# Expert outputs written straight to token order by a slot table, plain loads at the end, expert pairs in the two row halves

## The reference

```python
# attention: 8 heads of 64 rows each here, 2048 x 2048 scores a head
q, k, v = x @ Wq + bq, x @ Wk + bk, x @ Wv + bv
weights = softmax(einsum('bdsh,bdth->bdst', q, k) / SCALE)
x = layernorm(x + einsum('bdst,bdth->bdsh', weights, v) @ Wo + bo)
# experts: 64 of them, each token goes to 6, an expert takes the first 256 rows
shared = silu(g_s) * y_s @ w_shared_down
pos = cumsum(one_hot(flat_e))[...] - 1;  valid = pos < CAP            # CAP = 256
x_disp = zeros((E, CAP, C)).at[flat_e, pos].set(x_flat[token_ids], mode='drop')
out_r = (silu(g_r) * v_r) @ w_down                                    # one expert: 256 x 64 @ 64 x 512
y_ts = where(valid, out_r[flat_e, pos], 0)
x = layernorm(x + shared + (y_ts.reshape(N, TOPK, C) * w).sum(axis=1))
```

## Time and profile before

| | us |
|---|---|
| median of 3 runs | 1485.49 |
| lowest, highest | 1482.91, 1488.73 |
| the profiled execution | 1479.0 |
| its span in the trace | 1477.3 |
| PE busy in the span | 1280.4 |
| DVE, ACT, POOL busy | 1059.5, 875.6, 598.6 |

### The profile page before, as it was taken

The page is one execution under the profiler, slowest core; times in us unless marked ns, Lnnn a source line. Parts: engine busy times, 40 slices in busy tenths (PEclk is TensorE's granted clock), DMA queues, the critical chain, the costliest instruction groups (busy, mean ns, idle before and its releaser), DMA issues. The chain is left out here.

```text
span 1477.3 us, 24021 instructions
## 1 busy us (share of the span) xinstructions
PE 1280.4 (87%) x8064; PEld 1068.7 (72%) x8064; DVE 1059.5 (72%) x1964; ACT 875.6 (59%) x1573; POOL 598.6 (41%) x588
## 2 busy tenths in 40 slices
PE   7999899999999999999999999869999999960000
PEld 6888799898898998998988989847666666630000
DVE  4523688799898897997988989746665656645665
ACT  4421589788787887886887868712555555530000
POOL 0002223245244344343443442523444444447785
PEclk9999999999999999999999999979999999985555
DMA  9998111122122122121221221246999999966665
GB/s 353 351 375 290 52 32 37 46 79 81 43 82 86 33 92 78 60 85 61 79 89 37 81 87 39 76 150 202 292 321 333 330 328 332 323 209 192 205 204 159
DMA packets 158374, 235.79 MB, mean 160 GB/s; under 512 B 14000, under 2 KB 102576, under 8 KB 158256
## 3 DMA queue, kind: packets, MB, share of 16 engines
q1 hardware_dynamic: 131920, 147.50, 31.9%
q0 software_dynamic: 24576, 83.88, 16.1%
q10 hardware_dynamic: 1760, 2.88, 0.6%
HBM read 118.89 MB, written 109.05 MB: 154 GB/s over the span
## 5 line engine op out<-in xcount | busy, mean ns | idle before, releaser
L674 ACT ACTIVATE p_hi<-slot 128x512 fp32r<-128x512 f32 x512 | 279.3, 596 | 108.3 <-PE slot L1146 98.8
L514 POOL TENSOR_TENSOR p_lo<-prob,p_hi 128x512 fp32r<-128x512 f32 x128 | 165.5, 1293 | 436.2 <-ACT prob L676 432.4
L1159 PE MATMUL slot<-k_stack,q_stack 128*128 128x512 f32 x1024 | 300.5, 416 | 4.5 <-POOL v_pair L455 4.5
L687 ACT ACTIVATE prob<-prob,row_min 128x1024 f32<-128x1024 f32 x256 | 296.3, 1158 | 8.6 <-DVE prob L940 8.6
L919 DVE TENSOR_TENSOR p_lo<-slot,p_hi 128x512 fp32r<-128x512 f32 x384 | 250.8, 681 | 44.0 <-ACT p_hi L674 42.6
L1178 PE MATMUL pv_acc<-p_hi,v_pair 128*128 128x256 f32 x1024 | 265.6, 292 | 3.8 <-POOL p_lo L514 3.2
L1146 PE MATMUL slot<-ident,prob 128*128 128x128 f32 x2048 | 265.2, 272 | 1.2 <-ACT prob L687 1.2
L1178 PE MATMUL pv_acc<-p_lo,v_pair 128*128 128x256 f32 x1024 | 255.2, 282 | 0.0
L1146 PEld LDWEIGHTS slot<-ident,prob 128*128 128x128 f32 x2048 | 230.9, 140 | 1.7 <-DVE prob L940 1.6
L1178 PEld LDWEIGHTS pv_acc<-p_hi,v_pair 128*128 128x128 f32 x1024 | 193.0, 189 | 17.9 <-issue 8.4
L1178 PEld LDWEIGHTS pv_acc<-p_lo,v_pair 128*128 128x128 f32 x1024 | 192.8, 188 | 11.7 <-issue 3.4
(11 more groups left out here) (133 smaller groups left out, 2041.7 us busy)
## 6 DMA issues: line engine op xcount, KB each, us to landing
disp_hbm<-zeros SPq DMA_DIRECT2D x64, 512.0 KB, 6.5
rows<-disp_hbm SPq DMA_DIRECT2D x64, 512.0 KB, 7.3
y_hbm<-y_out POOLq DMA_DIRECT2D x64, 512.0 KB, 7.1
q_stack<-q_hbm SPq DMA_DIRECT2D x128, 128.0 KB
up_w<-in_L_ffn_w_up SPq DMA_DIRECT2D x64, 256.0 KB, 4.4
down_w<-in_L_ffn_w_down SPq DMA_DIRECT2D x64, 128.0 KB, 5.2
stage<-in_L_attn_x SPq DMA_DIRECT2D x8, 512.0 KB, 9.4
q_hbm<-q_hi SPq DMA_DIRECT2D x8, 512.0 KB, 3.8
```

What stands on the lines that cost most here:

```text
L514: e.tensor_tensor(p_lo[1][:, 2:4, :], prob[:, m % 2, :, (4 * u + 2) * P:(4 * u + 4) * P], p_hi[1][:, 2:4, :].bitcast(F32), ALU.subtract).t ...
L674: e.activation(p_hi[b][:, two, :], view[:, two, :], ACT.Copy).then_inc(a_phi, 1)
L687: e.activation(keys, keys, ACT.Exp, bias=row_min[:, me % 2, j, 1:2], scale=-1.0, accum_out=row_sum[:, me % 2, j, half:half + 1]).then_inc( ...
L1159: made = e.matmul(slot[:, n * BANK:(n + 1) * BANK], qs[:, part, j * P:(j + 1) * P], k_stack[:, ms % H, keys], start=part == 0, stop=part == 1)
```

## The change

The names of lines below are those of the changed kernel.

- `y_hbm` becomes 12288 rows in token order (token x 6 + k). While POOL scatters a tile's rows to `disp_hbm`, it also writes with six more indirect DMAs (`note_rows`, L526), each of 128 values of 4 bytes, the number token x 6 + k into `table_hbm` at the same slot. In all 96 such DMAs are added. The table is first filled with an index out of bounds. At n = 6 SP waits for all of them and loads the table; at n = 7 PE turns it and DVE copies it to `row_at`.
- `place` waits for the `note_rows` of the last tile too (`d_tabw`). `keep_slots` is gone.
- `y_hbm` needs zeros, since an overflowed row is never written: 48 DMAs of 512 KB, one in every fourth step of the attention. The zeros of `disp_hbm` move: none ahead of the q stores, 32 behind them, and 32 in the first 32 steps of the attention. POOL waits for them ahead of its first scatter.
- Two experts make a pair. `hid` and `down_w` hold the first in partitions 0 to 63 and the second in 64 to 127. The down products of both are formed in the odd round, in four calls that alternate between the halves. The copies to `y_out` and the stores come then for both.
- The store of an expert is two indirect DMAs (L619), so a pair has four.
- Weights are loaded eight experts ahead (the first eight when the attention ends), rows seven items ahead.
- In the tail SP loads `got` with one plain DMA for each tile of tokens (L475: 6 rows a partition, 1.57 MB), four ahead. ACT scales two of the six rows, POOL adds these two (`part`), DVE does four products and one addition. DVE writes the norm in place, and SP stores from `base`.

The diff, cut to its core:

```diff
-        y_hbm = hbm("y_hbm", (E * CAP, C))
+        table_hbm = hbm("table_hbm", (E * CAP, 1))
+        y_hbm = hbm("y_hbm", (T * TOPK, C))
...
-        NB, NY = 5, 3
+        NB, NY = 8, 4
...
-            takes += [("down", n)] if n >= 0 else []
+            if 0 <= n < NS:
+                takes += [("down", n)] + ([("table", 0)] if n == NS - 1 else [])
+            elif n >= NS and n % 2:
+                takes += [("down", n - 1), ("down", n)]
...
-            for g in range(NS):
-                pieces = zero_some(2)
+            for g in range(E // 2):
+                e.dma_start(disp_pieces[g], zero_row).then_inc(d_zero, 16)
...
+                if s < E // 2:
+                    e.dma_start(disp_pieces[E // 2 + s], zero_row).then_inc(d_zero, 16)
+                elif s % 4 == 2 and E <= s < E + 4 * NZ:
+                    e.dma_start(y_pieces[(s - E) // 4], zero_row).then_inc(d_yzero, 16)
...
             attention_over(e)
+            for g in range(NB):
+                load_weights(e, g)
...
+            def note_rows(t, k):
+
+                e.indirect_dma_start(
+                    table_hbm, bass.IndirectOffsetOnAxis(scat[:, k:k + 1], 0), row_of[:, t, k:k + 1], None,
+                    bounds_check=E * CAP - 1, oob_is_err=False).then_inc(d_tabw, 16)
...
-                if n >= NS:
-                    g, y = n - NS, n % NY
-                    e.wait_ge(v_y, g + 1)
-                    e.wait_ge(a_y, g + 1)
-                    e.dma_start(y_rows[g], y_out[y][:, :, :]).then_inc(d_y[y], 16)
+                if n >= NS and n % 2:
...
+                    for i in (n - 1, n):
+                        g, y = i - NS, i % NY
+                        for t in range(2):
+                            e.wait_ge((v_y, a_y)[t], g + 1)
+                            e.indirect_dma_start(
+                                y_hbm, bass.IndirectOffsetOnAxis(row_at[:, 2 * g + t:2 * g + t + 1], 0),
+                                y_out[y][:, t, :], None, bounds_check=T * TOPK - 1,
+                                oob_is_err=False).then_inc(d_y[y], 16)
...
+                if u >= NG:
+                    e.wait_ge(v_acc, ACC * (u - NG + 1))
+                    e.wait_ge(g_part, u - NG + 1)
+                e.dma_start(got[u % NG][:, :, :], y_tiles[u]).then_inc(d_got[u % NG], 16)
+                if u >= NG:
+                    store_out(u - NG)
...
                 e.wait_ge(d_scat, 16 * TOPK * (2 * c + j))
+                e.wait_ge(d_tabw, 16 * TOPK * (2 * c + j))
...
+                elif n >= NS and n % 2:
...
+                    for t in range(2):
+                        for at, slot in two:
+                            made = e.matmul(slot[:, t * BANK:(t + 1) * BANK], hid[pair % 2][at, t * P:(t + 1) * P],
+                                            down_w[pair % (NB // 2)][at, :], start=True, stop=True)
+                            if t:
+                                made.then_inc(p_down, 1)
```

251 lines of the change are left out of this document (145 added, 106 removed).

## The result

The changed kernel takes 1626.64 us (median, 1625.70 to 1629.48) against 1486.14 us for the kernel before it (1482.91 to 1488.73). The ratio is 1.095, 95% interval 1.092 to 1.098: slower by 9.5%. The forecast was 1621 us. The medians differ by 140.5 us.

What follows compares the result with a forecast made beforehand. PE was taken to bound attention and experts, POOL's gathers the tail. Expert stage +140, tail -32, start +5.5, attention +11 and transition +11 gave +136 on 1485.5, so 1621 us, range 1545 to 1670.

Steps and rivals of the forecast that it cites:

- expert stage: A closed loop through POOL's four DMAs and `up_lo` makes a pair 13.5 us: 419 us against 278.5, +140.
- tail: After the experts: 14.2 us a pair of tiles, loads held behind stores on SP; 130 us against 161.8, -32.
- transition: Between attention and experts: notes delay tile 14's root, and `place` of tile 15 waits for notes; +11, between 3 and 16.
- start of the attention: 32 zeros on SP ahead of the first `q_stack` loads make these land later; +5.5, between 0 and 9.
- attention: Added indirect DMAs on POOL hold back `p_lo` by 1.9 us at the end of six chunks; +11, between 0 and 20.
- D: Expert stage: time of a pair's eight down matmuls on two row halves, taken as 2.4 us, bounds 1.98 and 3.70.
- The step on the clock: Expert stage: PE's clock falls after 4.3 us idle in each pair, costing 1.7 us, bounds 0 and 2.25.
- The high clock with full overlap: Rival in the expert stage: no clock loss, halves fully side by side, 11.4 us a pair; 1559 us, chance 0.19.
- No overlap: Rival in the expert stage: the row halves do not run side by side, 14.8 us a pair; 1660 us, chance 0.19.
- The short pitch: Rival in the expert stage: POOL issues the `y_out` DMAs in 0.25 us, PE binds; 1444 us, chance 0.05.
- The rival with the loads in time: Rival in the tail: loads arrive in time, 23 us less than the forecast; 1598 us, chance 0.05.
- The second wait: Transition: `place` of tile 15 waits until the notes of tile 14 land at 1020.6, 12.6 us later.

Runs made afterwards that it cites:

- e_same: Changed kernel with POOL's writes put behind `up_lo`, one expert a round, and both experts of a pair multiplied from the first row half: 1502.2 us.
- e_order_noalt: Changed kernel with POOL's writes put behind `up_lo`, one expert a round, and down calls ordered A, A, B, B instead of alternating: 1442.21 us.
- e_filler: Changed kernel plus 32 extra matmuls of PE ahead of its wait for the late `up_lo` of each pair: 1549.0 us.
- e_order: Changed kernel with POOL's indirect writes put behind the `up_lo` they held up, one expert a round: 1443.87 us, ratio 0.974 to the kernel before.
- e_tail: Changed kernel with SP issuing both loads of a pair of tail tiles before the stores of the pair two back: 1604.24 us.
- e_trans: Changed kernel with the last tile's input loaded ahead of SP's twelve weight loads, and POOL's last roots ahead of tile 13's notes: 1612.21 us.
- e_again: The changed kernel itself run again, nothing altered: 1615.94 us.
- e_best2: Changed kernel with new orders in experts, transition and tail, and the 32 zero writes ahead of `q_stack` moved into the attention's first 32 steps: 1415.61 us.
- e_half_inds: Changed kernel writing only the first 128 rows of each expert, one indirect write instead of two: 1510.79 us.

## Why the prediction was right, point by point

**The sum.** In us:

| term | forecast | measured | by |
|---|---|---|---|
| expert stage | +140 | +144.5 | stage windows |
| tail | -32 | -32.0 | stage windows |
| transition | +11 | +29.8 | stage windows; 9 to 11 of it are ScalarE's stalls |
| start of the attention | +5.5 | +3.9 | PE's start 157.55 to 161.45 |
| attention | +11 | +0.7 | stage windows |
| sum | +136 | +147.0 | spans |

The sum is closer than its terms, and that is luck in part: the transition was 19 us too low and the expert stage 4.5, the attention 10 too high and the start 1.6. Against the medians, which differ by 140.5 us, the forecast is 5 us off, and as far from the changed kernel run again (1615.9) on the other side.

**Expert stage: right, by the steps given.** The links came out as added up: the copy starts when the down pair ends, POOL's DMAs at a pitch of 1.28, `up_lo` 1.28. Two sizes inside were off and cancel: D is 1.99 us at full clock where I took 2.4, and the clock costs 2.27 where I took 1.7. The step on D was "five of eight steps of 0.43"; the row halves overlap so far that eight matmuls take what four took in the earlier trace rows, which e_same and e_order_noalt show. The Trainium skill (TensorEngine Tiling (Array Packing), Key Properties: different tiles can load weights and multiply in parallel) had this right, and the trace agrees, eight matmuls in 1.99 us on two halves and 3.70 on one. The step on the clock took only 4 us of exposed work; the windows have a clock of 0.50 from 1305 to past 1310, 2.83 + about 2 us of it on the loop. With both corrected the sum is 9.4 + 2.0 + 2.2 = 13.6.

**The rivals there.** The high clock with full overlap (1559 us) failed by the clock alone: e_filler is that rival's kernel, at 11.4 us a pair. "No overlap" is out by 1.99. The short pitch is out by 1.28. What decided the sign was the price of an indirect DMA on POOL, taken from the earlier trace rows, and the place of POOL's instructions, not their sum: e_order has the same sum and is faster than the kernel before.

**Tail: right.** Forecast 14.2 us a pair of tiles, measured 14.75 (the start of a norm on DVE, 1530.96, to that of the next pair, 1545.71), with the wait for every second `got` at 3.07 to 3.16 us. The rival with the loads in time (3.9 us a pair less, 23 in all) is e_tail, which gave 22.4. That the whole came out at -32.0 is luck: the six pairs took 88.3 us (85.2 forecast) and the stretch from the first load to the first norm 28.8 (26), while the first load went out 7.7 us after the last down product (9.4) and only 5 us were left behind the last norm (9.7 forecast behind the last statistics).

**Transition: the mechanism was right, one size wrong.** The step "the bias (974.36) may itself be up to 5 us later; I take 4.5" is the one: the bias came at 990.61, 16 us later. SP's twelve weight loads, issued from 969.32 on, kept it until 984.80. The window of these loads in the changed kernel:

```profile
969.30:984.80 15.50, 11.21 (x23) 5.39 (x24) 4.07 (x6) 1.02 (x1) 1.67 (x2) 0.66 1.06 363
```

The DMA engines are full there and move 363 GB/s, 5.6 MB, of which the weights are 3.1. Most of the rest must be the six row loads of 512 KB that ACT issued from 963.77 to 967.58. In e_trans the same twelve loads, issued 9 us later, took 8.4 us (978.28 to 986.73) at 334 GB/s. So the step counted the bytes of its own queue and left out those that ACT's queue moves at the same time. The second wait, `place` of tile 15 behind the notes of tile 14, is there: in e_again DVE waits 4.30 us for them ahead of `place` at 1030.05 (1020.6 forecast), and PE stands 3.2 us behind it. Without ScalarE's stalls the term would have been about +19 to +21.

**Attention: the step failed.** It held that POOL would be 1.9 us late at the end of six chunks against a step of 5.7 to 6.25 us. PE waits 3.2 us in all for `p_lo` in the changed kernel, as in the kernel before. POOL's list at the place of the step:

```profile
471.74 0.97 POOL L526 DMA_INDIRECT table_hbm<-row_of,scat  x1 [0.31 <-issue]
...
473.99 1.29 POOL L577 TENSOR_TENSOR p_lo<-prob,p_hi 128x512 fp32r<-128x512 f32 x1
...
483.00 1.27 POOL L577 TENSOR_TENSOR p_lo<-prob,p_hi 128x512 fp32r<-128x512 f32 x1 [2.72 <-ACT prob L734]
```

`p_lo` ran at 473.99 instead of wherever its data would have let it, but the next was due only at 483.00: the step there is 9 us long, because PE has the output projection of the chunk in it. The two `p_lo` of the kernel before stood at 467.25 and 476.70, the second after 8.15 us of idle time. The pitch of 5.5 in the earlier trace rows is that of a step without chunk work, and the notes were put where there is some.

**Start: right in kind.** 32 zeros took SP 41.09 us, 1.28 each and not the 1.44 of the earlier trace rows; e_best2 shows that they are the cause.

## What to carry to other kernels

An engine that is busy for less than half of a stage can bound it, if in its order the work that the others wait for stands behind work that waits for them: follow the circle and add its links, then see whether a turn of it can be cut by letting the late work stand one round later, which here turned +9.5% into -2.6% with the same instructions. A stall of PE in such a circle can lengthen it: behind 4.48 us of idle time the up product and the down pair ran at half the clock, and as they are links too, each turn cost 2.27 us more. When the circle is opened, look for the next one: in e_order an engine with 0.24 us to spare in a turn was not the bound. When a load is moved behind others in a queue, price the bytes ahead of it together with those that the other queues move at that time.

## What was not expected of the hardware

- PE with 32 useless matmuls in each pair was 4.1% faster than without them (1549.0 to 1615.9 us), because the clock stayed at 1.00.
- Behind a stall of 2.0 us the clock fell to 0.50 for some 3 us in most turns of e_half_inds and in one of e_order (1.97 us), and stayed at 1.00 in a few turns of e_half_inds. Behind the waits of 0.8 to 1.5 us in e_order it stayed at 1.00.
- Two calls on one row half followed by two on the other take no longer than calls in turns: 1.99 us for eight matmuls of 64x512, and 3.70 if all are on one half.
- The changed kernel showed stalls of ScalarE worth 9 to 11 us in some groups of runs and not in others; its own executions within a group agree within 0.3%.
